# One score bank of a block attention: exponentials per head on ScalarE instead of shift, exponential and sum over the whole bank

## The reference

```python
q = ((x @ wq + bq) * HEAD_DIM ** (-0.5)).reshape(b, s, N_HEADS, HEAD_DIM)
k = (x @ wk + bk).reshape(b, s, N_HEADS, HEAD_DIM)
v = (x @ wv + bv).reshape(b, s, N_HEADS, HEAD_DIM)
scores = jnp.einsum('bqhd,bkhd->bhqk', q, k)
p = jax.nn.softmax(scores, axis=-1)
o = jnp.einsum('bhqk,bkhd->bqhd', p, v).reshape(b, s, d)
return o @ wo + bo
```

## Time and profile before

| | us |
|---|---|
| median of 3 runs | 879.84 (877.14 to 879.88) |
| the profiled execution | 873.75 |
| its span, first to last instruction | 872.0 |
| PE / PEld busy | 754.6 / 503.2 |
| DVE / ACT / POOL busy | 567.9 / 418.8 / 329.7 |
| mean granted TensorE clock | 0.935 |

### The profile page before, as it was taken

The page is one execution under the profiler, slowest core; times in us unless marked ns, Lnnn a source line. Parts: engine busy times, 40 slices in busy tenths (PEclk is TensorE's granted clock), DMA queues, the critical chain, the costliest instruction groups (busy, mean ns, idle before and its releaser), DMA issues. The chain is left out here.

```text
span 872.0 us, 19156 instructions
## 1 busy us (share of the span) xinstructions
PE 754.6 (87%) x7000; PEld 503.2 (58%) x7000; DVE 567.9 (65%) x1275; ACT 418.8 (48%) x1261; POOL 329.7 (38%) x424
## 2 busy tenths in 40 slices
PE   6999999798899999967777399999488888958996
PEld 5788877544333333345455288888366776446334
DVE  3565556437699999977697732232389887556474
ACT  3756656363574666225465100000077884545572
POOL 2222222126477887731253261100374553244001
PEclk9999999898699999988989589999879999989999
DMA  8112700000020000000001035652366420000001
GB/s 269 37 42 54 267 25 2 2 1 1 24 74 1 1 1 0 1 2 0 2 3 50 22 112 174 200 164 78 114 205 201 112 74 3 1 2 3 0 1 50
DMA packets 44893, 51.79 MB, mean 59 GB/s; under 512 B 7072, under 2 KB 40832, under 8 KB 44544
## 3 DMA queue, kind: packets, MB, share of 16 engines
q1 hardware_dynamic: 40256, 43.48, 16.1%
q0 software_dynamic: 1536, 4.20, 1.6%
q10 hardware_dynamic: 3008, 2.88, 1.0%
HBM read 45.31 MB, written 5.24 MB: 58 GB/s over the span
## 5 line engine op out<-in xcount | busy, mean ns | idle before, releaser
L1008 PE MATMUL r_u_ps<-r_t_in,l_same_head 128*128 128x512 f32 x124 | 69.6, 643 | 1.0
L976 POOL TENSOR_TENSOR r_q_in<-r_state,rec_q 128x512 f32<-128x512 f32 x62 | 68.1, 1098 | 0.0
L1807 ACT ACTIVATE a_prob<-a_s_ps,a_negmax 128x256 f32<-128x256 f32 x128 | 58.6, 483 | 18.8 <-DVE a_negmax L1843 18.8
L1417 ACT ACTIVATE a_prob<-a_s_ps,a_negmax 128x256 f32<-128x256 f32 x128 | 59.1, 487 | 17.7 <-DVE a_negmax L1479 17.7
L2420 PE MATMUL m_h_ps<-m_rowsT,l_w 128*128 128x256 f32 x256 | 58.6, 390 | 0.0
L1485 DVE COPY a_probT<-a_w_ps 128x512 f32<-128x512 f32 x48 | 31.4, 687 | 37.2 <-PE a_w_ps L1333 37.1
L2420 PEld LDWEIGHTS m_h_ps<-m_rowsT,l_w 128*128 128x128 f32 x256 | 50.3, 197 | 7.2
L2431 PE MATMUL m_y_ps<-l_w,m_hidden 128*128 128x256 f32 x240 | 53.9, 379 | 0.0
L2466 ACT ACTIVATE m_rowsT<-m_xt_ps,l_B_s,l_B_g 128x256 f32<-128x256 f32 x16 | 8.2, 560 | 93.2 <-PE m_xt_ps L2408 93.2
L2333 DVE TENSOR_SCALAR m_hidden<-m_h_ps,l_b 128x256 f32<-128x256 f32 x64 | 28.0, 480 | 37.8 <-PE m_h_ps L2420 37.8
L966 POOL TENSOR_TENSOR r_faded<-r_state,rec_both 128x256 f32<-128x256 f32 x62 | 39.8, 641 | 33.4 <-DVE r_state L945 33.4
(11 more groups left out here) (403 smaller groups left out, 1882.5 us busy)
## 6 DMA issues: line engine op xcount, KB each, us to landing
l_w<-in_B_w SPq DMA_DIRECT2D x16, 1024.0 KB, 5.8
a_ctxT<-in_ctxT SPq DMA_DIRECT2D x31, 256.0 KB, 2.9
a_ctx<-in_ctx SPq DMA_DIRECT2D x16, 256.0 KB, 2.8
expert_out<-m_y ACTq DMA_DIRECT2D x7, 256.0 KB, 5.7
all_X<-in_x SPq DMA_DIRECT2D x4, 256.0 KB, 5.5
l_b<-in_B_b SPq DMA_DIRECT2D x1, 1024.0 KB, 4.9
own_rows<-n_rows SPq DMA_DIRECT2D x2, 512.0 KB, 3.0
all_xnT<-own_rows SPq DMA_DIRECT2D x1, 1024.0 KB, 5.3
```

Source lines behind the costliest of these rows:

```text
L976: ins = nc.gpsimd.tensor_tensor(q_in[i % 2][m][:, :, :, :], twice(state[i % 2][m]), steps("q", 2 * i - 1, 2, m), ALU.mult)
L1008: nc.tensor.matmul(u_ps[m][:, :, :, :], same_head[:, :], t_in[m][:, :, :, :], start=False, stop=True).then_inc(u_mm[m], 1)
L1417: ins = nc.scalar.activation(prob[n % 2][:, r, m, :], s_ps[r][:, m, :], ACT.Exp, bias=negmax[n % 2][:, r, m:m + 1], accum_out=den[n % 2][: ...
L1807: ins = nc.scalar.activation(prob[n % 2][:, r, m, :], s_ps[r][:, m, :], ACT.Exp, bias=negmax[n % 2][:, r, m:m + 1], accum_out=den[n % 2][: ...
```

## The change

In stage a1 alone (`not bounded`), bank 3 of each unit takes another way. VectorE takes its maxima first, negated. ScalarE then reads the bank itself, one ACTIVATE for each of the 8 heads (64 columns), with the negated maximum as bias and the row sums as accumulator output. So bank 3 has no shift, no exponential over 512 columns and no sum on VectorE. Of unit u+1 the eight head-wise exponentials stand between the copies of unit u, as 3, 3 and 2. Banks 0 to 2 are worked as before. scores(u+1) now waits for three shifted banks and for the new semaphore `by_head`.

```diff
+        by_head = sc.sem("by_head") if not bounded else None
...
                     if u >= 1:
-                        pe.wait_ge(shifted_ready, ONE + 4 * u)
+                        pe.wait_ge(shifted_ready, ONE + WIDE * u)
+                        if not bounded:
+                            pe.wait_ge(by_head, ONE + 8 * u)
...
+                def exps_by_head(u, first, last):
+
+                    if first == 0:
+                        act.wait_ge(top_ready, ONE + 4 * u + 1)
+                        if u >= 2:
+                            act.wait_ge(pt_mm, ONE + 4 * (u - 1))
+                            act.wait_ge(rden_ready, ONE + 4 * (u - 1))
+                    for h in range(first, last):
+                        nc.scalar.activation(of_bank(u, 3)[:, h, :], s_ps[3][:, h, :], ACT.Exp, bias=top[:, 3, h:h + 1], accum_out=den[u % 2][:, 3, h:h + 1]).then_inc(by_head, 1)
...
-                for r in range(4):
+                if not bounded:
+                    exps_by_head(0, 0, 8)
+                for r in range(WIDE):
                     exps(0, r)
                 for u in range(NU):
                     for r in range(3):
                         take_transposed(u, r)
+                        if u + 1 < NU and not bounded:
+                            exps_by_head(u + 1, 3 * r, min(3 * r + 3, 8))
...
                 for u in range(NU):
                     if not bounded:
+                        maxima(u, 3)
                         maxima(u, 0)
                         maxima(u, 1)
-                    for r in range(4):
+                    for r in range(WIDE):
                         shift(u, r)
-                        if not bounded and r + 2 < 4:
-                            maxima(u, r + 2)
+                        if not bounded and r == 0:
+                            maxima(u, 2)
                     sums(u, 0)
                     for r in range(4):
-                        if r + 1 < 4:
+                        if r + 1 < WIDE:
                             sums(u, r + 1)
                         reciprocals(u, r)
```

More of the change, by code:

```diff
@@ L1980, in batch_attention_stage @@
     bounded = limit is not None
+    WIDE = 4 if bounded else 3
     with Scope(nc, stage) as sc:
@@ L2087, in exps @@
                 def exps(u, r):
-                    act.wait_ge(shifted_ready, ONE + 4 * u + r + 1)
+                    act.wait_ge(shifted_ready, ONE + WIDE * u + r + 1)
                     if u >= 2:
@@ L2118, in _ @@
                     if u + 1 < NU:
-                        for r in range(1, 4):
+                        for r in range(1, WIDE):
                             exps(u + 1, r)
@@ L2126, in maxima @@
                     dve.wait_ge(s_mm, ONE + 4 * u + r + 1)
-                    nc.vector.tensor_reduce(top[:, r, :], s_ps[r][:, :, :], AX.X, ALU.max).then_inc(top_ready, 1)
+                    if r == 3 and u >= 1:
+                        dve.wait_ge(by_head, ONE + 8 * u)
+                    nc.vector.tensor_reduce(top[:, r, :], s_ps[r][:, :, :], AX.X, ALU.max, negate=(r == 3)).then_inc(top_ready, 1)
                 def shift(u, r):
@@ L2132, in shift @@
                     else:
-                        dve.wait_ge(top_ready, ONE + 4 * u + r + 1)
+                        dve.wait_ge(top_ready, ONE + 4 * u + r + 2)
                     if u >= 1:
-                        dve.wait_ge(exp_done, ONE + 4 * (u - 1) + r + 1)
+                        dve.wait_ge(exp_done, ONE + WIDE * (u - 1) + r + 1)
                     if bounded:
@@ L2141, in sums @@
                 def sums(u, r):
-                    dve.wait_ge(exp_done, ONE + 4 * u + r + 1)
+                    dve.wait_ge(exp_done, ONE + WIDE * u + r + 1)
                     nc.vector.tensor_reduce(den[u % 2][:, r, :], of_bank(u, r), AX.X, ALU.add).then_inc(den_ready, 1)
                 def reciprocals(u, r):
-                    dve.wait_ge(den_ready, ONE + 4 * u + r + 1)
+                    if r < WIDE:
+                        dve.wait_ge(den_ready, ONE + WIDE * u + r + 1)
+                    else:
+                        dve.wait_ge(by_head, ONE + 8 * (u + 1))
                     if u >= 2:
```

## The result

The changed kernel takes 880.98 us (median, 875.1 to 888.89), the kernel before, run beside it, 877.22 (874.81 to 881.02). The ratio is 1.0035, 95% interval 1.0018 to 1.0051: slower by about 3.1 us. One of the 22 executions, that of 888.89 us, ran in a slower state that some executions show, and the ratio leaves it out. The profiled execution has a span of 879.9 us against 872.0, but that is no measure of the change: an execution of the same changed kernel later had 873.6, with the same stage a1. The other stages differ by several us from one execution to the next: over the twelve profiled executions of this document stage a1 begins at 428.3 to 434.1 us, and 396.7 to 403.7 us follow behind it. So I read the stage by itself, from the first scores matmul to the start of the last `add`. That was 431.06 to 472.06 = 41.00 us. Now it is 431.85 to 476.22 = 44.37 us, or 3.37 more.

The account below looks back on a forecast made before the run. VectorE was taken to bound stage a1, with ScalarE the new bound after the change. GpSimd's unit 3 coming 1.31 us late gave 873.75 + 1.31 = 875.06 profiled, with 0.15% more 881.2 us; range 878.0 to 885.4.

Parts of the forecast that it names:

- Price of the pair: ScalarE, stage a1: a 64-column ACTIVATE with bias plus its accumulator read costs 0.30 us, eight cost 2.40 us a unit.
- Rival A: Pair on ScalarE cheap, 0.11 us at its lower bound: result -2.3 us, 877.5 us; chance 0.15.
- B: Rival: pair on ScalarE not overlapped, 0.50 us each: +7.2 us, 887.1 us; chance 0.06.
- The new bound: Units 1 to 3: ScalarE becomes the bound, and VectorE's saved 1.2 us a unit turn into waits for exponentials.
- Cycle: Loop from copy 0 over ScalarE, VectorE, GpSimd and the transposes to the next copy 0: 8.17 us, against VectorE's 7.48.
- GpSimd's starts: Starts of GpSimd's four units: unit 1 late by 0.55 us, unit 3 late by 1.31 us against before.
- Unit 0: GpSimd's first unit starts 0.60 us earlier, at 437.90, as one shift on VectorE goes.
- the new order: VectorE's maxima in new order, with the negation: costed at nothing, same instructions and sizes.
- The sum of the order of work: Stage a1's delay by the start of GpSimd's unit 3, passed on to the end: +1.31 us.
- rival C: TensorE's clock stays at the low level to the stage's end: +6.7 us beside 1.3, 887.8 us; chance 0.07.
- the way from GpSimd's unit 3 to the last `add`: End of stage a1: nothing changes there, as no pairs are left.
- The prediction's own sign of being wrong: Wrong if VectorE runs without gaps, GpSimd's units are under 7.5 us apart, or granted clock is 0.5 after 444 us.

Follow-up runs that it names:

- one_fill: Changed kernel with 4 throwaway matmuls on TensorE ahead of values(0) only, against the kernel before: stage a1 43.72 us, ratio 0.9986.
- warm_after: Changed kernel with throwaway matmuls behind scores(0), ahead of values(0) and of unit 3's transposes, run twice: stage 41.95 us both times; ratio to before 1.0046, then 1.0017.
- wide_bank: Changed kernel with bank 3's eight pairs replaced by one 512-column exponential after copy 2, no maximum subtracted, no sums: stage 41.57 us, ratio to the kernel before 1.0009.

## Why the prediction was right, and what it missed

- Price of the pair: 0.30 forecast, 0.29 measured. Rival A (0.11) and B (0.50) are out by that row alone.
- The new bound: VectorE's saved 1.20 us a unit turned into waits for ScalarE's exponentials, 1.58 + 0.32 in unit 1. Cycle 8.17 forecast, 8.15 to 8.17 measured wherever the clock was 1.00.
- GpSimd's starts: forecast at 437.9, 446.5, 454.7 and 462.9, measured, taken from the same start of the stage, at 438.0, 446.6, 455.8 and 463.9. Units 0 and 1 are as worked out. Units 2 and 3 are 1.0 late by the low clock, and the last `add` by another 1.0.
- Unit 0: 0.60 earlier forecast, 0.48 measured. The maxima begin with bank 3, whose last matmul is the last: VectorE starts 1.31 us after the first matmul instead of 1.19. I had costed the new order at nothing; it costs 0.12 once.
- The sum of the order of work: +1.31 forecast. Measured, 3.37 less the 1.98 of the two new low stretches = +1.39. Held against both kernels at the full clock it is 0.94; the other 0.45 is the first low stretch, in unit 0, which both kernels have (unit 0 to 1 is 8.62 with it, 8.16 without). It was hidden behind VectorE before and now lies on the chain through copy 0 (2.25 instead of 1.8 us after GpSimd). The sum contained it, in its 2.25.
- The step that was mis-sized: rival C, the clock, with 0.07 and as a matter of a whole stage, "In part (one unit) it costs under 2 us". It came in part, every time, at 1.98 us. I had the wait that causes it in hand (TensorE done at 443, copy 3 at 444.5) and dismissed it by a wait of 0.96 us that had left the clock up, when the new one was 2.04. The other term put at nothing is the way from GpSimd's unit 3 to the last `add`: "nothing changes" there, and it took 11.53 us instead of 10.50. The prediction's own sign of being wrong, a granted clock of 0.5 after 444 us, came. With the clock as measured its sum gives +3.3 us (1.31 + 1.98), not +1.3, and a loss of 0.35 to 0.37% is just over what can be told from no change, where 0.79 of the chance lay within it.
- That 881.2 stands so near to 880.98 is luck, two errors that cancel: the base was 2.6 us too high and the change some 2 us too small. The median of the three runs before was 879.84, that of 22 runs 877.22. The size of the change is the fair comparison, 0.15% forecast against 0.35%: the way it went and the mechanism of its first 1.3 us were right, the size was not. The range's lower end, 878.0, is also not quite rival A's end as the text says, which is 877.5.

Shown are the price, the ScalarE cycle, and that a filled wait removes the low clock in unit 2. Open is why the last unit's stretch comes: filling removes it as well, together with the others, but no run fills that place alone, and the wait ahead of it was shorter than before (1.37 against 1.68). Open too is what beside the length of the wait brings the stretch in unit 2, which came behind 1.18 us in the kernel with the wide exponential. And open is what moves the rest of the execution by several us, with one_fill's and the first warm_after's totals off their stages by more than their intervals.

## What to carry to other kernels

When an engine is full, ask how far behind it the next loop is before giving its work away: here GpSimd, TensorE and the copies had only tenths of a us of slack, so 4.8 us of saved VectorE work could bring some 1.6, by the estimate above. Work moved to an engine with idle time still costs its full length if it is put in front of what others wait for; the place counts as much as the price. And idle time on TensorE in the middle of a stage is to be costed twice, once as a wait and once as the matmuls behind it at half the clock. A look at the longest wait is not enough for that: here the clock fell behind 1.18 us in one kernel and stayed behind 1.68 in another.

## What the runs showed of the hardware

- A wait of 2.04 us of TensorE, behind 4.10 us of transposes that had begun at the low clock, was followed by a stretch at the 1.2 GHz level; 64 small matmuls then took 2.01 us instead of 1.21. The same wait cut to 0.49 us by throwaway matmuls left the clock at 1.00. The low stretch was there in both profiles of the changed kernel.
- No single wait length parts the cases of this document: the clock was at 0.50 behind a wait of 1.18 us (wide_bank, ahead of values(0)) and within 2 us behind one of 1.37 us (changed kernel, ahead of the last transposes), and at 1.00 behind waits of 1.03 and 1.68 us (kernel before, the same two places).
- ScalarE's recorded lengths grow in a stretch without idle time while the steps stay: the pair's ACTIVATE reads 0.31 at first and 0.37 as the eighth, an exponential over 512 columns 0.69 instead of 0.62, with 0.29 and 0.52 from start to start all along. Steps are what to add up.
